# Experts' lists with the tile as innermost index, compared with a written-out table of digit numbers

## What is computed

```python
N = B * S                                   # 4096 tokens
k = max(MIN_CAPACITY, ceil(N * CAPACITY_FACTOR / E))    # 1024 per expert
xt = x.reshape(N, D)
scores = jax.nn.softmax(xt @ Wr, axis=-1)
G, idx = jax.lax.top_k(scores.T, k)
X_in = xt[idx]
h = jax.nn.gelu(jnp.einsum('ekd,edh->ekh', X_in, W1) + b1[:, None, :], approximate=False)
X_e = jnp.einsum('ekh,ehd->ekd', h, W2) + b2[:, None, :]
contrib = (G[..., None] * X_e).reshape(E * k, D)
out = jnp.zeros((N, D), dtype=x.dtype).at[idx.reshape(-1)].add(contrib)
```

## Time and profile before

| what | value |
| --- | --- |
| median of three runs | 1182.62 us |
| the profiled execution's own time | 1187.13 us |
| its span in the profile | 1185.3 us |
| PE (TensorE matmuls) busy | 939.8 us (79%) |
| DVE (VectorE) busy | 818.0 us (69%) |
| ACT (ScalarE) busy | 655.7 us (55%) |
| POOL (GpSimd) busy | 422.0 us (36%) |
| experts' phase | 655 to about 874 us of the span |

### The profile page before, as it was taken

One profiled execution on the slowest core, in us unless ns is written; L12 is line 12 of the kernel. 1 busy time (PEld: TensorE's weight loads), 2 busy tenths in 40 slices (PEclk: granted clock), 3 DMA queues, 4 the chain that ended last, 5 costly groups with the idle time before them and its releaser, 6 DMA issues. The chain is left out here.

```text
span 1185.3 us, 24918 instructions
## 1 busy us (share of the span) xinstructions
PE 939.8 (79%) x8605; PEld 646.8 (55%) x8605; DVE 818.0 (69%) x1701; ACT 655.7 (55%) x2201; POOL 422.0 (36%) x334
## 2 busy tenths in 40 slices
PE   6679898898999999899672489887508988884886
PEld 3346556575656666576561366555304555553664
DVE  5777776869687776867478845113344799879997
ACT  3476685867778676867424234232106888873432
POOL 2323542434333242333100277778830222222211
PEclk9898999999999999999855589898858999997887
DMA  7665453454635444454220223325850000000000
GB/s 208 160 174 142 108 136 101 125 134 101 159 99 144 114 122 117 128 133 110 59 67 1 73 48 89 87 71 129 225 140 1 1 2 1 1 2 0 27 19 27
DMA packets 102148, 106.27 MB, mean 90 GB/s; under 512 B 19264, under 2 KB 71984, under 8 KB 102080
## 3 DMA queue, kind: packets, MB, share of 16 engines
q1 hardware_dynamic: 94400, 96.74, 30.5%
q0 software_dynamic: 7680, 8.66, 3.8%
HBM read 30.68 MB, written 16.99 MB: 40 GB/s over the span
## 5 line engine op out<-in xcount | busy, mean ns | idle before, releaser
L857 POOL TENSOR_TENSOR qk_cos<-qk_raw,const 128x512 f32<-128x512 f32 x128 | 181.8, 1421 | 304.7 <-ACT qk_raw L609 304.6
L595 ACT ACTIVATE prob<-psS,neg_max 128x96 f32<-128x96 f32 x512 | 167.4, 341 | 78.8 <-DVE neg_max L690 77.5
L564 PEld LDWEIGHTS psO<-probT,v_windows 96*64 96x64 f32 x2048 | 71.6, 140 | 139.2 <-ACT probT L669 117.8
L456 PE MATMUL psQ<-a_xnT,weights 128*128 128x512 f32 x250 | 144.2, 661 | 3.2 <-ACT a_xnT L641 2.0
L564 PE MATMUL psO<-probT,v_windows 96*64 96x64 f32 x2048 | 89.5, 231 | 41.4 <-ACT probT L669 40.8
L705 DVE TENSOR_TENSOR qk_roped<-qk_cos,qk_swapped 128x512 f32<-128x512 f32 x128 | 120.6, 942 | 0.3
L696 DVE TENSOR_TENSOR qk_swapped<-qk_swapped,const 128x512 f32<-128x512 f32 x128 | 90.8, 709 | 21.4 <-DMA qk_swapped<-qk_raw 20.3
L1517 POOL DMA_INDIRECT ex_rows<-rows,ex_index x64 | 69.1, 1080 | 102.1 <-DMA ex_index<-lists 83.5
L595 ACT ACTIVATION_READ_ACCUMULATOR prob<-psS,neg_max 128x1 f32 x512 | 105.1, 205 | 0.0
L669 ACT COPY probT<-psT 96x512 f32<-96x512 f32 x128 | 76.7, 599 | 47.0 <-PE psT L544 47.0
L609 ACT COPY qk_raw<-psQ 128x512 f32<-128x512 f32 x125 | 74.0, 592 | 42.5 <-PE psQ L456 39.7
(11 more groups left out here) (353 smaller groups left out, 1958.4 us busy)
## 6 DMA issues: line engine op xcount, KB each, us to landing
qk_swapped<-qk_raw SPq DMA_DIRECT2D x512, 64.0 KB, 2.0
v_windows<-v_tok SPq DMA_DIRECT2D x32, 384.0 KB, 4.4
v_windows<-v_tok SPq DMA_DIRECT2D x32, 256.0 KB, 3.6
sums<-zeros SPq DMA_DIRECT2D x32, 256.0 KB, 2.5
mod<-mod_rows SPq DMA_DIRECT2D x12, 512.0 KB, 6.4
ex_w<-in_L_ffn_W SPq DMA_DIRECT2D x16, 256.0 KB, 3.1
v_windows<-v_tok SPq DMA_DIRECT2D x32, 96.0 KB, 2.1
rows<-rt_h SPq DMA_DIRECT2D x8, 256.0 KB, 2.4
```

Of the source, the lines that this page charges most:

```text
L456: last = nc.tensor.matmul(bank, k.wqkvT[:, col:col + P], xnT[:, :], start=True, stop=True)
L564: ins = nc.tensor.matmul(psO[D * j:D * j + D, i * P + a * HALF:i * P + (a + 1) * HALF], vw[:, par, a, t, hd], probT[:, 2 * j + i, a * HALF ...
L595: last = nc.scalar.activation(prob[:, s, 2 * j + i, :], psS[:, s, j, i * KW:(i + 1) * KW], ACT.Exp, bias=nmax[:, s, 2 * j + i:2 * j + i + ...
L857: nc.gpsimd.tensor_tensor(rcos[:, half, :], raw[:, half, :], k.const[:, K_COS:K_COS + T], ALU.mult).then_inc(cos_done, 1)
```

## The change

The tables `digit`, `high`, `low` and `low_of` have their axes in another order: the tile is now the innermost index, where it was the digit number (in `digit`, the expert of the group). The comparison no longer reads one digit repeated over 32 places against `iota`; it reads the digits of consecutive tiles, repeated for each digit number, against `each`, a table of 32 digit numbers x 32 tiles in bf16 that holds each number 32 times. It is written once, into space of `y` that expert 1's output takes later. The multiplication by the tile number reads `iota` along the tiles. The matmuls read one tile out of tables in which the tile is innermost, so that their columns are 32 elements (64 bytes) apart. Number and size of the comparisons, multiplications and matmuls stay.

```diff
-        digit = sb("ex_digit", [P, 2, GROUPS, NT, GROUP], BF16)
+        digit = sb("ex_digit", [P, 2, GROUPS, GROUP, NT], BF16)
         iota = sb("ex_iota", [P, NT], BF16)
-        high = sb("ex_high", [P, 2, NT, GROUP, SPLIT], BF16)
-        low = sb("ex_low", [P, 2, NT, GROUP, SPLIT], BF16)
-        low_of = sb("ex_low_of", [P, 2, 2, NT, GROUP, SPLIT], BF16)
+        high = sb("ex_high", [P, 2, GROUP, SPLIT, NT], BF16)
+        low = sb("ex_low", [P, 2, GROUP, SPLIT, NT], BF16)
+        low_of = sb("ex_low_of", [P, 2, 2, GROUP, SPLIT, NT], BF16)
...
+        each = y[:, 1, :, :].rearrange("p s c -> p (s c)").bitcast(BF16)[:, 0:SPLIT * NT].rearrange("p (l t) -> p l t", t=NT)
...
-                    last = nc.tensor.matmul(psL[g % 2][0:LISTED, 0:2 * LISTED], high[:, g % 2, t, :, :], low_of[:, g % 2, :, t, :, :],
+                    last = nc.tensor.matmul(psL[g % 2][0:LISTED, 0:2 * LISTED], high[:, g % 2, :, :, t].rearrange("p e l -> p (e l)"),
+                                            low_of[:, g % 2, :, :, :, t].rearrange("p v e l -> p (v e l)"),
                                             start=(t == 0), stop=(t == NT - 1))
...
             weights1.clear()
+            own.mark(nc.vector.tensor_copy(each, k.const[:, K_IOTA:K_IOTA + SPLIT].unsqueeze(2).to_broadcast([P, SPLIT, NT])))
             dve.wait_ge(ranked, 1)
...
                 own.mark(nc.vector.tensor_copy(digit[:, i, :, :, :],
-                                               digit_i[:, i, :].rearrange("p (t g e) -> p g t e", g=GROUPS, e=GROUP)))
+                                               digit_i[:, i, :].rearrange("p (t g e) -> p g e t", g=GROUPS, e=GROUP)))
...
             def one_hot(out, i, g, tiles):
-                n = (tiles.stop - tiles.start) * GROUP
-                return nc.vector.tensor_tensor(out[:, tiles, :, :].rearrange("p t e l -> p (t e) l"),
-                                               digit[:, i, g, tiles, :].rearrange("p t e -> p (t e)").unsqueeze(2).to_broadcast([P, n, SPLIT]),
-                                               iota[:, 0:SPLIT].unsqueeze(1).to_broadcast([P, n, SPLIT]), ALU.is_equal)
+                n = tiles.stop - tiles.start
+                return nc.vector.tensor_tensor(out[:, :, :, tiles],
+                                               digit[:, i, g, :, tiles].unsqueeze(2).to_broadcast([P, GROUP, SPLIT, n]),
+                                               each[:, :, tiles].unsqueeze(1).to_broadcast([P, GROUP, SPLIT, n]), ALU.is_equal)
...
-                nc.vector.tensor_tensor(low_of[:, buf, 1, :, :, :].rearrange("p t e l -> p t (e l)"),
-                                        low[:, buf, :, :, :].rearrange("p t e l -> p t (e l)"),
-                                        iota[:, :].unsqueeze(2).to_broadcast([P, NT, LISTED]), ALU.mult).then_inc(weighed, 1)
+                nc.vector.tensor_tensor(low_of[:, buf, 1, :, :, :].rearrange("p e l t -> p (e l) t"),
+                                        low[:, buf, :, :, :].rearrange("p e l t -> p (e l) t"),
+                                        iota[:, :].unsqueeze(1).to_broadcast([P, LISTED, NT]), ALU.mult).then_inc(weighed, 1)
```

More of the change, by code:

```diff
@@ L1359, in phase_experts @@
         n = Weights.WIDTH
-        spare_f = spare(low_of[:, :, :, :, :, :], "p g v t e l -> p (g v t e l)")
+        spare_f = spare(low_of[:, :, :, :, :, :], "p g v e l t -> p (g v e l t)")
         weights1 = Weights(nc, k, ctx, psL, [spare_f[:, i * n:(i + 1) * n] for i in range(3)]
-                           + [spare(high[:, :, :, :, :], "p g t e l -> p (g t e l)")[:, 0:n]])
+                           + [spare(high[:, :, :, :, :], "p g e l t -> p (g e l t)")[:, 0:n]])
         own = Tally(sem("own"))
@@ L1433, in _ @@
                 wait(act, listed, g - 1)
-                nc.scalar.activation(low_of[:, g % 2, 0, :, :, :].rearrange("p t e l -> p (t e l)"),
-                                     low[:, g % 2, :, :, :].rearrange("p t e l -> p (t e l)"), ACT.Copy,
+                nc.scalar.activation(low_of[:, g % 2, 0, :, :, :].rearrange("p e l t -> p (e l t)"),
+                                     low[:, g % 2, :, :, :].rearrange("p e l t -> p (e l t)"), ACT.Copy,
                                      scale=k.const[:, K_TOKEN:K_TOKEN + 1]).then_inc(weighed, 1)
```

## The result

With the change the kernel takes 1189.28 us (median of six runs, 1186.3 to 1194.85), before it 1182.07 (1178.5 to 1186.11). The ratio is 1.007, 95% interval 1.0048 to 1.0093: slower by 0.5 to 0.9%. The forecast was 1174.7 in a range of 1171 to 1184.

A forecast was written before the change was run, and what follows sets the result against it. From 674.95 us on, GpSimd issuing 128 indirect DMAs one after another was taken to bound the experts' phase. An earlier start (2.57 us) and less contention (5.4) sum to 7.9: 1182.6 - 7.9 = 1174.7 us, range 1171 to 1184.

The forecast's parts named there:

- The queue of GpSimd as the bound: Experts' phase from 674.95 us: GpSimd issuing 128 indirect DMAs one after another sets the time.
- the hold by VectorE: Expert 0's eight gathers wait for VectorE operations with two SBUF inputs: 7.2 us lost, 1.8 after the change.
- The rule for the hold: About 0.12 us into a gather GpSimd waits for the running VectorE operation; the gather ends about 0.82 us behind it.
- VectorE's pace and the added cast: List building: `low` and multiplication each save 1.07 us, a half of `high` 0.53; the new table's cast costs nothing.
- The cover of 1.84 us: VectorE's wait for TensorE's ranks, to hide the table's cast of at most 1.22 us.
- ScalarE ends the wait of the first block: First list: ScalarE's copy, 2.11 us with its steps, becomes what the matmuls wait for; VectorE needs 2.01.
- TensorE's part: List matmuls with columns 64 bytes apart: a block of 32 was taken to stay at 3.59 us.
- p: Time of one block of 32 list matmuls, 3.59 us before; gain gone from 6.0 us on.
- the doubling (7.2): List matmuls at twice their time, if the cache line rule held: block 7.2 us, kernel 4.6 us longer than before.
- the bound of 7.9: Upper limit for a list matmul block, from transposes of 128 f32 columns at 246 ns each: 7.9 us.
- The formula of the queue: First scatter: y ready at 702.5 + 4 (p - 3.59), queue arrives at 704.3 + (p - 3.59); the later decides.
- the case that came true: Rival of other sign: TensorE's list blocks reach 6.0 us or more, 1182.6 to 1190 us, chance 0.13.

The follow-up runs named there:

- runs of 2: Changed kernel with tables in runs of 2 tiles innermost, matmul columns 4 bytes apart instead of 64: 1174.41 us, 0.9912 of the kernel before.

## Why the prediction was wrong

- **The queue of GpSimd as the bound**: right. The length of every kernel's phase followed what reached this queue, and when. In runs of 2, expert 1's gathers begin 26.88 us into the phase, where it was 36.68: the first gather came 4.1 us earlier, and the hold by VectorE shrank by 5.7. Forecast were 2.57 and 5.4; 1.4 us of the first difference is the ranks' matmuls, which ran at the upper clock in this execution and not in the one before. The rule for the hold, 0.12 us into a gather, was a little too strict: the gather from 686.33 in the kernel before should have waited by it and did not.
- **VectorE's pace and the added cast**: right, 1.23 and 0.69 us for the pace, 0.05 us for the cast. The cover of 1.84 us that the cast relied on was a matter of the rank matmuls' clock; with the quicker ones of this execution the cast of 0.63 us only just fitted. The digits' casts cost 0.19 us together, inside the 0 to 0.25.
- **ScalarE ends the wait of the first block**: right, in every kernel of the fast pace.
- **TensorE's part, the step that failed**: "I take p unchanged: at the 1.2 GHz level a moving column is due only each 0.83 ns, half as often as at the other level." That took it that a column with 16 bytes to itself comes within those 0.83 ns, which no row showed. It took 1.7 to 1.8 ns at either clock. The block was 7.3 us, between the doubling (7.2) and the bound of 7.9 that stood in the text, and not 3.59. Four such blocks turned a forecast gain of 7.9 us into a loss of 7.2. The Trainium skill (Advanced Engine Details and Errata, section "SBUF Cachelines"), which I weighed and set aside, was right about the place of the step: one column in 16 bytes is dear (7.61 us a block, with two 3.96). Its full performance with two hits in a line holds here at 1.2 GHz to within 10% (123 against 112 ns) and fails at 2.4 GHz (117 against 62 ns); the measurement decides.
- **The formula of the queue**: right in its form. With p = 7.3 it gives y at 702.5 + 4 x 3.7 = 717.3, 5.1 us later than the scatter of before. Measured in the phase were 7.1 at the first scatter (63.95 against 56.86). Expert 0's first layer at a mean clock of 0.74 (2.4 us more) was not in it, nor the 0.8 us from the finished y (721.14) to the scatter (721.98), and the quicker ranks of this execution hide 1.4 us of the whole: 5.1 + 2.4 + 0.8 - 1.4 = 6.9. That layer's clock is not shown to be the layout's doing, so its 2.4 us may belong to this execution alone.
- **The chances**: the case that came true, blocks of 6.0 us or more, stood at 0.13, with its sign and its time (1182.6 to 1190) as measured. It should have weighed about as much as the forecast: for an unchanged block spoke only that no row showed otherwise, and a bound of 2.2 times had been read from the trace.

## What to carry to other kernels

A layout has two sides. Before an index is made innermost for VectorE, look at the step that it leaves for TensorE's moving operand, and keep at least four bf16 columns in 16 bytes (here a run of two tiles); VectorE needed no more than that run of two. Two columns in 16 bytes were as good for this kernel (1175.11 us against 1174.41), whose blocks run mostly at the lower clock level. And where an engine's work is cheaper by a microsecond, ask what queue receives it: here GpSimd's gathers gained more from VectorE's shorter operations than from the earlier start.

## What the runs showed of the hardware

- A moving column of bf16 that has 16 bytes for itself cost 1.7 to 1.8 ns at 0.50 and at 1.00 of the clock. Two in 16 bytes cost 116 to 123 ns for 128 at 0.50 and 117 at 1.00. Four in 16 bytes took 112 ns at 0.50 and 62 ns at 1.00.
- With spread columns TensorE was busy for 28.6 us in one piece at 0.50 throughout; with two columns in 16 bytes blocks of 15.3 us rose to 1.00 on the way. Started at 1.00 behind dense matmuls, a spread block stayed there from 671.50 to 677.00 us and then fell back (0.50 from 678.00 on). Why the clock did so is not shown.
- At 0.50, spread stationary columns (64, 32 bytes apart) added only 15 to 16 ns to a pair, spread moving ones (128, 64 bytes apart) 110.
- A VectorE comparison of 2048 elements took 1.22 us with all operands in bf16 and advancing by one in the innermost index, in runs of 32 and of 2 alike; 2.29 us with one value repeated innermost, and also with one input in f32.
- A gather by indirect DMA that begins inside a VectorE operation with two SBUF inputs ends 0.82 us behind the end of that operation (2.94, 2.02 and 2.02 us beside three additions). Beside one with an input in PSUM it took 0.95 us, and 0.94 in two cases where it began within 0.03 us of the operation's start.
